# Summing the scaled keys on GpSimd instead of with one product of ones per tile, in a graph layer of attention, message passing and experts

## What is computed

```python
xn = _layernorm(x, axis=-1)
k = _split_heads(seq @ wk.T, B, S)          # seq = xn[None], 4 heads of 64
v = _split_heads(seq @ wv.T, B, S)
k = _layer_norm(k, ln_k_g, ln_k_b)
v = _layer_norm(v, ln_v_g, ln_v_b)
kv = jnp.einsum('bhsd,bhse->bhde', k, v) / S
ga = jnp.einsum('bhsd,bhde->bhse', q, kv)
return ga @ wo.T + bo
```

## Time and profile before

| | |
|---|---|
| time, median of 3 runs | 1108.15 us (1106.34 to 1108.5) |
| span of the profiled execution (no other time of it is given) | 1109.2 us |
| TensorE busy | 1053.5 us, 95% |
| VectorE busy | 887.2 us, 80% |
| ScalarE busy | 691.9 us, 62% |
| GpSimd busy | 747.1 us, 67% |

### The profile page before, as it was taken

One profiled execution on the slowest core, in us unless ns is written; L12 is line 12 of the kernel. 1 busy time (PEld: TensorE's weight loads), 2 busy tenths in 40 slices (PEclk: granted clock), 3 DMA queues, 4 the chain that ended last, 5 costly groups with the idle time before them and its releaser, 6 DMA issues.

```text
span 1109.2 us, 23680 instructions
## 1 busy us (share of the span) xinstructions
PE 1053.5 (95%) x7990; PEld 993.3 (90%) x7990; DVE 887.2 (80%) x1409; ACT 691.9 (62%) x1075; POOL 747.1 (67%) x703
## 2 busy tenths in 40 slices
PE   4897999999999999999999999999799999999995
PEld 2465899999999999999999989997599999999995
DVE  7877888888999888888899972488777777777773
ACT  2562667766666666666666643664467777777663
POOL 5447777777777777777777756540147777777764
PEclk9998999999999999999999998999899999999998
DMA  7211445545444544444455420222458988988972
GB/s 243 77 55 37 137 142 143 143 144 140 143 141 137 146 140 141 142 142 142 142 143 143 144 60 25 71 86 56 153 171 232 229 224 228 225 229 211 240 192 22
DMA packets 118495, 159.74 MB, mean 144 GB/s; under 512 B 20536, under 2 KB 91020, under 8 KB 118412
## 3 DMA queue, kind: packets, MB, share of 16 engines
q0 software_dynamic: 31104, 66.28, 26.0%
q1 hardware_dynamic: 86748, 91.60, 25.3%
q10 hardware_dynamic: 560, 0.79, 0.3%
HBM read 142.42 MB, written 18.17 MB: 145 GB/s over the span
## 4 chain that ended last, share of the span: by engine, by line
PE 87%; DVE 7%; issue 2%; ACT 2%; DMA 1%; DVEq 0%; POOLq 0%; POOL 0%; SPq 0%; ACTq 0%
PE ps L1595 25%; PE ps L1786 16%; PE ps L1606 15%; PE ps L1549 8%; PE ps L1798 8%; PE ps L1650 4%; PE ps L1523 2%; PE ps L1662 2%; PE ps L1675 2%; PE ps L1725 1%; PE ps L1773 1%; DVE st L979 1%; PE ps L1532 1%; PE ps L1533 1%; PE ps L1516 1%
## 5 line engine op out<-in xcount | busy, mean ns | idle before, releaser
L1595 PE MATMUL ps<-fr 128*128 128x256 f32 x2352 | 306.6, 287 | 3.2 <-DVE fr L1041 3.2
L1595 PEld LDWEIGHTS ps<-fr 128*128 128x128 f32 x2352 | 288.9, 192 | 4.1 <-DVE fr L1041 4.0
L590 POOL DMA_INDIRECT big<-xn_rows,srcs x200 | 219.6, 1098 | 61.3 <-issue 61.3
L590 POOL DMA_INDIRECT hgx<-xn_rows,srcs x192 | 210.5, 1096 | 58.5 <-issue 58.5
L742 ACT ACTIVATE h1f<-ps,b 128x512 f32<-128x512 f32 x196 | 124.2, 684 | 167.3 <-PE ps L1549 166.4
L1606 PEld LDWEIGHTS ps<-oh,big 128*128 128x128 f32 x1568 | 190.7, 192 | 8.7 <-DVE big L1177 0.5
L1786 PE MATMUL ps<-fr 128*128 128x256 f32 x1536 | 191.5, 285 | 2.7 <-issue 1.4
L1786 PEld LDWEIGHTS ps<-fr 128*128 128x128 f32 x1536 | 188.2, 193 | 3.2 <-issue 1.7
L1606 PE MATMUL ps<-oh,big 128*128 128x96 f32 x1568 | 189.0, 274 | 0.4 <-DVE big L1186 0.4
L1041 DVE TENSOR_TENSOR fr<-h1f,fr 128x1024 fp32r<-128x1024 f32 x98 | 120.1, 1225 | 51.8 <-ACT fr L745 51.7
L662 POOL DMA_INDIRECT out<-xnT,idx x64 | 117.9, 1842 | 50.3 <-issue 35.3
(11 more groups left out here) (219 smaller groups left out, 1418.5 us busy)
## 6 DMA issues: line engine op xcount, KB each, us to landing
big<-in_w SPq DMA_DIRECT2D x128, 256.0 KB, 4.3
rbf<-in_rbf SPq DMA_DIRECT2D x98, 256.0 KB, 2.9
big<-in_w SPq DMA_DIRECT2D x32, 512.0 KB, 4.3
xn_rows<-xn SPq DMA_DIRECT2D x26, 128.0 KB, 2.6
big<-xn_rows,srcs POOLq DMA_INDIRECT x200, 3.2
xn_rows<-hgx SPq DMA_DIRECT2D x24, 128.0 KB, 2.2
hgx<-xn_rows,srcs POOLq DMA_INDIRECT x192, 3.2
x_nodes<-in_x SPq DMA_DIRECT2D x2, 768.0 KB, 9.2
```

Source lines behind the costliest of these rows:

```text
L590: pool.indirect_dma_start(hg[i % HB][:, s, :], None, xn_d[:, :], bass.IndirectOffsetOnAxis(srcs[:, col:col + 1], 0))\
L1595: last = mm(ps[:, 2 + 4 * p + s // 2, (s % 2) * D:(s % 2 + 1) * D], h1s[p][a][:, c, s * P:(s + 1) * P], W2s[b][:, c, :], start=c == 0 and ...
```

## The change

GpSimd gets a third instruction per tile, `add_k(t)`, between `scale_v(t)` and `add_biases(t)`: it adds the tile's scaled keys to `ksum`, 128x256, element by element. `ksum` is zeroed among the constants and lies in `hgx`, in memory that gather 3 overwrites later. TensorE's product of `ones` and `khs` per tile is gone; after the last `sum_kv` one product of `ones` and `ksum` adds over the partitions, into the same bank, and increments `s_mx` itself. A new semaphore `s_ks` counts the adds: `add_k(t)` waits for the add before it and for `scale_k(t)`, `scale_k(t)` waits for `add_k(t - 2)`, since it writes into the buffer which that one reads, and the last product waits for all adds. Gather group 3 waits for that product.

```diff
--- before.py
+++ after.py
@@ -214,6 +214,7 @@
         xt2 = [oflat[i % 2][:, i // 2 * D:(i // 2 + 1) * D].rearrange("p (c q) -> p c q", c=DC) for i in range(4)]
         khs = [oflat[i][:, 0:2 * (P + 2)].rearrange("p (j c) -> p j c", j=2) for i in range(2)]
         vhs = [oflat[i][:, 2 * (P + 2):2 * (P + 2) + D] for i in range(2)]
+        ksum = part(hgx, 1024, 2, P)
         hflat = h1f[:, :, :].rearrange("p c e -> p (c e)")
         MX = EV + ET * D * 5
         kvt = part(big, MX, DC, P)
@@ -300,6 +301,7 @@
         s_kh = sem("k_scaled")
         s_vh = sem("v_scaled")
         s_khp = sem("kv_summed")
+        s_ks = sem("k_added")
         s_mx = sem("mix_products")
         s_mv = sem("mix_vector")
         s_rbf = [sem(f"rbf_in{i}") for i in range(2)]
@@ -512,6 +514,7 @@
                                     base=LAST, pattern=[[0, 1]], channel_multiplier=-1))
             for p in range(2):
                 link(pool.memset(khs[p][:, :, P:P + 2], 1.0))
+            link(pool.memset(ksum, 0.0))
             link(pool.iota(spare[:, :], [[0, CAPB], [P, SB // P]], base=NP, channel_multiplier=1,
                            allow_small_or_imprecise_dtypes=True))
             pool.sem_inc(s_const, 1)
@@ -533,6 +536,10 @@
                                    kvc[:, t, D:2 * D].rearrange("p (h d) -> p h d", d=HD),
                                    kvr[:, t * 8 + 4:t * 8 + 8].unsqueeze(2).to_broadcast([P, 4, HD]), ALU.mult)\
                     .then_inc(s_vh, 1)
+            def add_k(t):
+                pool.wait_ge(s_kh, t + 1)
+                pool.wait_ge(s_ks, t + 2)
+                pool.tensor_tensor(ksum, ksum, khs[t % 2][:, :, 0:P], ALU.add).then_inc(s_ks, 1)
             def centre_wkv():
                 pool.wait_ge(s_wsum, 1)
                 heads = wkv[:, :, :].rearrange("p c (h d) -> p (c h) d", d=HD)
@@ -571,8 +578,10 @@
             link(pool.tensor_tensor(cb[:, 0, :], cb[:, 0, :], cb[:, 1, :], ALU.add))
             edge_tables()
             edges_left()
+            pool.sem_inc(s_ks, 2)
             for t in range(NT):
                 scale_v(t)
+                add_k(t)
                 add_biases(t)
 
 
@@ -585,6 +594,8 @@
                     pool.wait_ge(s_msg, n0 + max(i + 1, HB))
                     if type(n0) is not int:
                         pool.sem_inc(s_turn, 1)
+                    elif i == 3:
+                        pool.wait_ge(s_mx, 1)
                     for s in range(ET):
                         col = i * ET + s
                         pool.indirect_dma_start(hg[i % HB][:, s, :], None, xn_d[:, :],
@@ -1024,6 +1035,7 @@
             def scale_k(t, p):
                 dve.wait_ge(s_kvr, t + 1)
                 dve.wait_ge(s_khp, t + 1)
+                dve.wait_ge(s_ks, t + 1)
                 dve.tensor_tensor(khs[p][:, :, 0:P].rearrange("p j (h d) -> p j h d", d=HD),
                                   kvc[:, t, 0:D].rearrange("p (j h d) -> p j h d", j=2, d=HD),
                                   kvr[:, t * 8:t * 8 + 4].rearrange("p (j h) -> p j h", j=2).unsqueeze(3)
@@ -1529,9 +1541,9 @@
                 pe.wait_ge(s_kh, t + 1)
                 pe.wait_ge(s_vh, t + 1)
                 for c in range(DC):
-                    mm(ps[:, 4 + c, 0:P + 1], vhs[p][:, c * P:(c + 1) * P], khs[p][:, c, 0:P + 1], start=start, stop=stop)
-                mm(ps[:, 6, 0:D].rearrange("p (c d) -> p c d", c=DC), ones[:, :], khs[p][:, :, 0:P],
-                   start=start, stop=stop).then_inc(s_khp, 1)
+                    last = mm(ps[:, 4 + c, 0:P + 1], vhs[p][:, c * P:(c + 1) * P], khs[p][:, c, 0:P + 1],
+                              start=start, stop=stop)
+                last.then_inc(s_khp, 1)
             transpose_xn(0, 0, 0, s_tp, s_xn)
             transpose_xn(1, 1, 0, s_tp, s_xn)
             pe.wait_ge(s_cen, 1)
@@ -1565,8 +1577,8 @@
                 if t == NT - 3:
                     pe.wait_ge(s_wlow, 1)
                     up(0, 0, 0)
-            pe.wait_ge(s_khp, NT + 2)
-            pe.sem_inc(s_mx, 1)
+            pe.wait_ge(s_ks, NT + 2)
+            mm(ps[:, 6, 0:D], ones[:, :], ksum.rearrange("p c d -> p (c d)"), start=True, stop=True).then_inc(s_mx, 1)
 
 
             def mix_a1():
```

## The result

The changed kernel takes 1116.42 us (median of 4, 1114.81 to 1117.9) against 1108.12 us: a ratio of 1.0076, 95% interval 1.0064 to 1.0088, so it is slower by some 8.3 us. I had forecast 1106.9 us, with 1112 as the upper end and "slower" at 0.23. The forecast was wrong in its sign and its range. The profiled execution of the changed kernel took 1114.81 us at a span of 1113.0, 3.8 us over the profiled span of before.

What follows compares the result with a forecast made beforehand. TensorE's tile-after-tile work bounds the stretch to the last projection, then VectorE's chain the drain. Stretch -4.0, drain +2.3, clock +0.4 give -1.3 us on the 1109.2 span; forecast time 1106.9 us, range 1103 to 1112.

Steps and rivals of the forecast that it cites:

- The stretch (-4.0): First sum to last projection's end: products removed, VectorE becomes the bound, 42.3 to 38.3 us, 4.0 us saved.
- The drain (+2.3, and +0.4 for the clock): Last projection to gates: GpSimd's added instructions delay sum_kv(22), costing 2.3 us net; lower TensorE clock costs 0.4.
- the lower row: In the drain, GpSimd's time per instruction taken near the lower rows: 0.78 us, between 0.71 and 0.91.
- my upper bound of +4.2: Drain's worst cost in us, from a range of +0.8 to +4.2.
- the clock term: In the drain, TensorE idles more with half its work gone, so `up` slows: 0.4 us added.
- The second: Rival: shared port becomes the bound in stretch and drain; up to +5.7, 1113.9, half-way 1111.5; chance 0.20.
- The third: Rival: gathers lose over 2.8 us of lead, last message waits, 1 to 2 us more, 1108.4; chance 0.05.
- The first: Rival: TensorE keeps the beat, drain costs its least; -5.7, 1102.5, half-way 1104.7; chance 0.27 with the fourth.
- The final product: End of the drain: the one product left is covered before the gates, by 0.4 to 0.8 us.
- The lock read literally: GpSimd and VectorE times add up in full: stretch 50.4 us, kernel some 1120; 0.02 of the second rival's chance.

Runs made afterwards that it cites:

- b_add: Kernel before with the 25 GpSimd adds and their waits added, TensorE's products per tile kept; ratio 1.0036 (0.9989 to 1.0083).
- a_split: Changed kernel with GpSimd adds for tiles 0 to 15 only, TensorE's products kept for 16 to 24, 94 filler instructions; ratio 1.0014 (0.998 to 1.0049).
- b_fill53_q: Kernel before with 53 one-instruction semaphore increments, awaited by nobody, in GpSimd's list, on the third chip; 1112.85 us, ratio 1.0039.
- a_fill75_q: Changed kernel with 75 one-instruction semaphore increments, awaited by nobody, in GpSimd's list, on the third chip; 1113.03 us, ratio 1.0038.
- a_noadd: Changed kernel with the 25 adds left out, their waits kept, 25 filler instructions to keep the list's length; ratio 1.0107, on a disturbed edge stage.
- a_fill75: Changed kernel with 75 filler increments in GpSimd's list, earlier run on a chip with a disturbed edge stage; ratio 1.0025 (0.9983 to 1.0067).

## Why the prediction was wrong

**The stretch (-4.0) was right as far as TensorE goes.** It gave 3.5 us (last projection at 82.62 against 86.08; I had said 82.3), and TensorE's share of it was right too: 6.4 of the 6.5 us when nothing is put in its place. The mechanism was the one named, an add starting behind its tile's scale_k and meeting VectorE's next work. Only the place of it was broader: make_xn took 0.40 to 0.82 us, about half of the time undisturbed, while Newton steps were hit instead. The beat between projections was 2.58 us on average (2.17 to 3.15) for the 2.55 that I gave. Some luck is in how close that is: VectorE's busy time rose by 3.3 us and not by 4.9, and for the other 2.1 us of the stretch it had no instruction at work, which my sum did not have.

**The drain (+2.3, and +0.4 for the clock) is the step that failed.** It grew by 5.4 us (20.45 to 25.90). By the prediction's own marks:

| from | to | before | after | forecast change | measured |
|---|---|---|---|---|---|
| last projection's end | scale_k(17) | 4.30 | 5.52 | 0 | +1.2 |
| scale_k(17) | sum_kv(22) | 9.45 | 13.24 | +2.7 | +3.8 |
| sum_kv(22) | gates | 6.70 | 7.14 | 0 | +0.4 |

The first row is a hole in the stretch's gain. Before, VectorE kept up with TensorE and waited for it: scale_k(16) started at 86.54, 0.5 us behind the last projection. Now VectorE is the bound, and at the last projection's end it still had an ssq and a Newton step for tile 16 to do (0.30, 0.65 and 0.54 us from 83.17 on): scale_k(16) starts at 84.98, 2.4 us behind. Of the 3.5 us that TensorE's projections won, VectorE's queue had won 1.6 at scale_k(16) and 2.2 at scale_k(17). I took the end of the projections for the end of the stage, when I had just said that they would no longer bound it. The experiments agree: b_add, whose projections end as before, has 4.06 us in this row, and a_split, with no adds in the drain, 6.18.

In the second row I had followed GpSimd alone, 15 instructions of 0.78 us behind scale_k(17). They took 12.6 us, 0.84 each, between my mid and my upper end. But the first part of it is VectorE's: from scale_k(17) to scale_k(19) it needed 4.46 us where before it needed 2.55, with 0.6 of waiting in that. I wrote "VectorE waits more here", and so took the lower row; in the first half of the drain it hardly waits, it is the bound. From scale_k(19) to sum_kv(22) it is 8.78 us for 6.90, and there TensorE waits for scale_v. The whole is over my upper bound of +4.2. The last row of the table is the clock term: I gave 0.4 for `up`, it took 0.8 more (2.06 for 1.28 us), less the 0.43 of the removed product. I had put the lower clock down to TensorE's missing work alone, but b_add, which keeps that work, has 0.71 in the drain and 2.27 us for `up`.

The sum of the node stage was therefore +2.0 at the gates (106.53 to 108.52) where I had -1.3. The gates at 105.0 to 105.5 and the first gather near 105 were wrong with it. The timed cost of this part is 4.2 us (2.8 to 5.6), while the profiles show 2.0 to 2.7 at the gates (against before and b_fill53_q), 1.3 to 1.4 at the last message (against before), and 2.4 of span for a_fill75_q. The interval's lower end touches them, and before's profile is some 3 us over its median; whether another 1 to 2 us lie in a later stage or in the spread stays open.

**The cost that no term and no rival had** is the other half, 3.8 to 4.3 us, 700 us behind the change. A longer list moved an instruction transfer into the gap between GpSimd's copy and its first scatter, in a stage in which TensorE then waited for GpSimd's gathers (2.5 us). I had counted the new instructions by their busy time only. That the transfer is there is seen, in all profiles with the gap and in none without it; that GpSimd waits for that load, and is not stopped by something that comes with it, is inferred.

**The rivals.** The second (the shared port as the bound, half-way 1111.5) came nearest: the sum alone, without the list, is at 1113.03, by its mechanism in the drain and not in the stretch. The whole, 1116.42, is over that rival's upper bound (1113.9) too, as the list was in none. The third, late gathers, did not occur: the lead shrank by 0.8 us (first gather 2.8 later, gates 2.0) where I had 2.7. The first fell with the drain. The final product was covered as said, by 1.9 us and not 0.4 to 0.8. The lock read literally (the Trainium skill, SBUF — State Buffer, Who interferes with whom) would give the stretch 50.4 us; it took 38.82, so there the trace does not agree with full addition. For single instructions in the drain it agrees: Newton instructions of 0.18 us that meet an add or a bias add of 0.68 to 0.72 us take 0.63 to 0.67.

## What to carry to other kernels

Before work is moved to an idle engine, follow the queue of the engine that feeds it as well: an operation that starts when its producer ends lands on that engine's next instructions, and where these are short (0.18 us here) one of them can take nearly the length of the moved one (0.68 us). Judge each stage by itself, as the same edit gave 3.5 us where TensorE was the bound and took 5.4 where it was not; and when the bound moves to another engine, count from where that engine's queue stands. An ablation that keeps the waits of what it removes is not free of them, as a_noadd showed. And when a change alters an engine's instruction count, compare the late stages too: a difference with no cause in the code there may be the place of an instruction load. Fillers of no meaning can show it, one run that brings it to the old kernel and one that takes it from the new.

## What the runs showed of the hardware

- An instruction-queue transfer in front of GpSimd's scatter went with 5.0 to 5.6 us of idle time in six profiles, for 1.06 to 1.07 us in the eight without it. 53 added instructions brought it and 75 more (128 in all) took it away. Brought to the kernel before, it cost 0.39% (0.25 to 0.52).
- TensorE's granted clock in the drain up to sum_kv(22) was 0.88 before, 0.69 without products and adds, 0.71 with both, and 0.57 to 0.62 with the adds alone. The four products of a sum took 0.71 us at its upper level (2.4 GHz) and 1.20 to 1.23 at its lower (1.2 GHz), behind idle times of 1.1 to 2.5 us that came one after the other from 83.4 us on. At the gates it differs from one execution to the next: with one and the same node stage the 24 products took 3.14 us (after, a_fill75_q) or 4.62 (a_fill75).
- A VectorE instruction of 0.18 us took 0.63 to 0.67 us beside a GpSimd add. Over a whole stretch the two did not exclude each other in full: 38.8 us, where their undisturbed times add up to 50.4 (the prediction's estimate).
